# Second attention of a two-block transformer kernel: a tile's normalisation statistics taken one step, their aggregate two steps, behind its residual addition

## The reference: what is computed

```
x = x + jnp.tanh(g_xattn[0]) * _L0_xattn_ref(_layernorm(x, axis=-1), ctx_1024, ...)
x = x + jnp.tanh(g_ffn[0]) * _L0_ffn_ref(_layernorm(x, axis=-1), ...)
x = x + jnp.tanh(g_xattn[1]) * _L1_xattn_ref(_layernorm(x, axis=-1), ctx_1024, mask, ...)
x = x + jnp.tanh(g_ffn[1]) * _L1_ffn_ref(_layernorm(x, axis=-1), ...)

def _layernorm(x, axis=-1, eps=1e-05):
    m = jnp.mean(x, axis=axis, keepdims=True)
    v = jnp.var(x, axis=axis, keepdims=True)
    return (x - m) / jnp.sqrt(v + eps)
```

## Time and profile before

| | before |
|---|---|
| median of 3 runs | 753.41 us (750.35 to 755.98) |
| the profiled execution, its own time | 759.83 us |
| its span | 758.3 us |
| PE busy | 549.0 us (72%) |
| DVE busy | 416.8 us (55%) |
| POOL busy | 330.2 us (44%) |
| ACT busy | 231.6 us (31%) |
| mean granted TensorE clock | 0.832 of full |

### The profile page before, as it was taken

How to read it: one execution, slowest core, us unless ns; L and a number is a source line. 1 busy time by engine, 2 the same in 40 slices (tenths; PEclk the granted TensorE clock), 3 DMA queues, 4 the chain that set the end, 5 groups by cost and what they waited for, 6 DMA issues and landing times.

```text
span 758.3 us, 16967 instructions
## 1 busy us (share of the span) xinstructions
PE 549.0 (72%) x5388; PEld 433.3 (57%) x5389; DVE 416.8 (55%) x1474; ACT 231.6 (31%) x411; POOL 330.2 (44%) x412
## 2 busy tenths in 40 slices
PE   1587957615699999972798887777861388999950
PEld 1356645501289999862354676666650166999950
DVE  4785386997523333314896467878568511222215
ACT  0221001123044444442622454454531021223210
POOL 6212104777535656634500000070747676666650
PEclk9967695865799999996799997786775699999995
DMA  7911000123222222412755164352324113222219
GB/s 199 269 42 32 26 14 30 49 96 99 74 75 82 77 79 74 140 45 68 238 185 175 51 167 109 108 159 51 70 64 129 46 54 103 79 81 77 72 56 311
DMA packets 70254, 74.97 MB, mean 99 GB/s; under 512 B 12216, under 2 KB 58552, under 8 KB 70120
## 3 DMA queue, kind: packets, MB, share of 16 engines
q1 hardware_dynamic: 55240, 49.64, 23.6%
q0 software_dynamic: 9968, 21.88, 9.2%
q10 hardware_dynamic: 4976, 2.53, 1.2%
HBM read 45.62 MB, written 28.29 MB: 97 GB/s over the span
## 4 chain that ended last, share of the span: by engine, by line
PE 51%; DVE 24%; POOL 8%; issue 8%; DMA 6%; ACT 1%; SPq 1%; POOLq 0%; DVEq 0%; ACTq 0%
PE PS L802 47%; POOL xs L543 5%; DVE XN L1406 3%; DVE stats L1385 3%; DMA work<-ys 3%; DVE X L1380 2%; PE PS L983 2%; DVE work L1845 2%; DVE work L1380 1%; POOL work L591 1%; DVE rtmp L1380 1%; DVE mv L1388 1%; DVE nwt L1380 1%; PE PS L1144 1%; POOL work L598 1%
## 5 line engine op out<-in xcount | busy, mean ns | idle before, releaser
L543 POOL DMA_INDIRECT xs<-pack,adr_i x80 | 78.2, 977 | 194.3 <-ACT pack L1219 138.5
L554 POOL DMA_INDIRECT ys<-work x136 | 132.6, 975 | 33.2 <-issue 33.2
L802 PE MATMUL PS<-w,work 128*128 x1088 | 137.4, 281 | 6.5 <-issue 6.4
L802 PEld LDWEIGHTS PS<-w,work 128*128 128x128 f32 x1088 | 129.4, 195 | 11.5 <-issue 10.2
L802 PE MATMUL PS<-work,w1h 128*128 128x256 f16 (+1 forms) x576 | 97.8, 271 | 3.4 <-issue 2.0
L802 PE MATMUL PS<-work 97*64 97x256 f16 (+5 forms) x608 | 75.7, 317 | 13.8 <-DVE work L1512 7.5
L1380 DVE TENSOR_TENSOR work<-PS,work 128x128 f32<-128x128 f32 (+3 forms) x82 | 32.0, 392 | 94.9 <-PE PS L802 50.6
L802 PE MATMUL PS<-work,w1l 128*128 128x256 f16 (+1 forms) x288 | 78.1, 272 | 0.0
L1277 ACT ACTIVATE work<-PS,b 128x256 f32<-128x256 f32 x128 | 50.3, 475 | 77.0 <-PE PS L802 77.0
L802 PEld LDWEIGHTS PS<-work 97*64 97x64 f16 (+2 forms) x608 | 57.7, 165 | 24.7 <-DVE work L1512 10.8
L802 PE MATMUL PS<-ones 128*128 128x512 f16 x195 | 50.7, 418 | 25.7 <-DVE rows_i L1642 12.4
(11 more groups left out here) (288 smaller groups left out, 858.8 us busy)
## 6 DMA issues: line engine op xcount, KB each, us to landing
work<-ys SPq DMA_DIRECT2D x12, 512.0 KB, 6.0
work<-xs SPq DMA_DIRECT2D x32, 130.0 KB
work<-xs SPq DMA_DIRECT2D x60, 65.0 KB
k_parts<-work SPq DMA_DIRECT2D x24, 128.0 KB, 2.1
w<-k_parts SPq DMA_DIRECT2D x8, 384.0 KB
work<-k_parts SPq DMA_DIRECT2D x32, 96.0 KB
work<-q_parts SPq DMA_DIRECT2D x8, 384.0 KB
work<-q_parts SPq DMA_DIRECT2D x32, 96.0 KB
```

The lines of the kernel that those rows point to most:

```text
L543: g.indirect_dma_start(xs[l], bass.IndirectOffsetOnAxis(adr_i[:, k, T:T + 1], 0), pack_of(l, c)[:, s, k, :].bitcast(U32), None)\
L554: g.indirect_dma_start(ys[l], bass.IndirectOffsetOnAxis(xin[:, q, u, :].bitcast(U32)[:, D:D + 1], 0), yrow[:, q, u, :], None).then_inc(ff[ ...
L802: return t.matmul(o, lhsT, rhs, start=start, stop=stop, skip_group_check=True)
```

## The change

`norm_scale` is cut in two: the statistics, and the inverse square root (`norm_root`, unchanged in itself). In the second attention the statistics of a tile are no longer taken by the group. Behind the residual addition of tile `T` VectorE now issues the `bn_aggr` of tile `T-2` and the `bn_stats` of tile `T-1`, each once. When the step of "norm" comes, only what is left of the group is done (`bn_stats` of the last tile, `bn_aggr` of the last two), and then `norm_root`. Two new semaphores, `x3_stats` and `x3_mv`, order them. The other stages call `norm_scale` as before.

```
                 for T in range(t.start, t.stop):
                     ins = v_.bn_aggr(mv[:, T, :], stats[:, T, :])
                 link(ins)
+                norm_root(t)
+
+            def norm_root(t):
+                w = t.stop - t.start
                 x, y, z = nwt[:, 0, 0:w], rstd[:, t], nwt[:, 1, 0:w]
...
+            taken, kept = [0], [0]
+
+            def take_stats(stop):
+                for T in range(taken[0], stop):
+                    dve.wait_ge(x3_done, T + 1)
+                    v_.bn_stats(stats[:, T, :], X[:, T, 0:D]).then_inc(x3_stats, 1)
+                taken[0] = max(taken[0], stop)
+
+            def keep_stats(stop):
+                for T in range(kept[0], stop):
+                    dve.wait_ge(x3_stats, T + 1)
+                    v_.bn_aggr(mv[:, T, :], stats[:, T, :]).then_inc(x3_mv, 1)
+                kept[0] = max(kept[0], stop)
...
                 if 0 <= T < NT:
                     dve.wait_ge(o_ps, T + 1)
                     tt(X[:, T, :], X[:, T, :], PS[:, 6, 0:DE], ALU.add).then_inc(x3_done, 1)
+                    keep_stats(T - 1)
+                    take_stats(T)
...
                 for k in route_at("norm", g):
                     dve.wait_ge(x3_done, group(1, k).stop)
-                    norm_scale(group(1, k))
+                    take_stats(group(1, k).stop)
+                    keep_stats(group(1, k).stop)
+                    dve.wait_ge(x3_mv, group(1, k).stop)
+                    norm_root(group(1, k))
                     route_lg(1, k)
```

More of the change, by code:

```diff
@@ L287, in build @@
         x_plus = sem("x_plus")
+        x3_stats, x3_mv = sem("x3_stats"), sem("x3_mv")
         scat = [[sem(f"scat{l}_{u}") for u in range((4, 2)[l])] for l in range(2)]
```

## The result

The changed kernel takes a median of 749.62 us (743.84 to 757.14, 20 executions); the kernel before, executed again beside it, takes 755.44 us (750.35 to 760.13, 20 executions). The ratio is 0.9939 with a 95% interval of 0.9917 to 0.9960, that is 4.6 us faster, between 3.0 and 6.3; by the two medians it is 5.8. Forecast were 4.07 us, 749.3 us after, and "within 1%" with 0.86. The forecast held. That 749.3 lies so close to 749.62 is partly luck: it was counted from 753.41, the median of three executions, and with twenty the kernel before stands 2 us higher.

What follows compares the result with a forecast made beforehand. GpSimd's 32 scatters were taken to bound the kernel from chunk 4 on, so three groups of five counted: 1.09 + 1.39 + 1.59 = 4.07 us. From 753.4 us that gave 749.3 us, range 747.5 to 751.

Steps and rivals of the forecast that it cites:

- What a group frees: VectorE at each full group's norm: 2.34 us of statistics shrink to 0.485, freeing 1.86 us.
- What a pair costs: One inserted bn_stats and bn_aggr on VectorE: 0.265 us if they overlap as in the burst, 0.425 if not.
- Plain steps cover the pairs: Steps 17 to 20: VectorE waits for TensorE, so pairs are covered, at the tightest all but 0.03 us.
- First group: Norm before step 13: TensorE gains 0.4 us at once, VectorE's maximum 1.55; 1.09 us remain at step 16's heads.
- Second and third group: Second: 1.39 us gained by step 24's heads; third: 1.59 us by the first scatter of chunk 4.
- The waits: TensorE's heads in steps 13, 21 and 29 wait 0.5, 0.9 and 1.6 us; steps 16 and 24 keep some 3.
- GpSimd bounds the end: From chunk 4, 32 back-to-back scatters bound the stage, so nothing is counted for groups 3 and 4.
- Every pair is paid: Rival: no inserted pair is covered or overlaps, costing 8.5 us against 5.6 gained; 2.9 us slower, 756.3 us; chance 0.10.
- the change frees nothing: Rival: TensorE's half-clock stretches lengthen by as much as VectorE gives; 753 to 755 us; chance 0.06.
- Another wait takes the place: Rival: ScalarE's copy limits TensorE after all three norms, each giving 0.43 us; 752.1 us; chance 0.12.
- The clock gives more: Rival: shorter waits keep TensorE at full clock behind norms, 1.5 us more per stretch, 744.7 us with all three; chance 0.20.

Runs made afterwards that it cites:

- three pairs: The changed kernel with every inserted bn_stats and bn_aggr of the plain steps issued three times; 755.66 us, ratio 1.0000 to the kernel before.
- second profile of the change: The changed kernel itself, executed again as the measure for the runs beside it; 751.27 us, ratio 0.9909 to the kernel before.
- groups 3 and 4 alone: The kernel before with only the last two groups (tiles 24 to 31) taking statistics behind the residuals; 756.46 us, ratio 1.0028.
- groups 0 to 2 alone: The changed kernel with only tiles 0 to 23 taking statistics behind the residuals, the last two groups keeping bursts; 750.75 us, 0.9935 of the kernel before.
- the products: TensorE multiplies ones into a free bank during waits: on the changed kernel 747.89 and 747.20 us, on the kernel before 752.80 us.

## Why the prediction was right, point by point

**What a group frees.** Forecast 1.86 us, measured 1.80 in each of three groups. The remaining stretch is 0.54 us and not 0.485: the two aggregates last 0.30 together and start 0.21 behind the statistics, where 0.276 and small gaps had been put. Nothing in it was of another kind.

**What a pair costs.** Forecast 0.265 where it is on the path, measured 0.26 in steps 16 and 24, three times the same with three pairs, and 0.45 for a pair and a lone `bn_stats` together against 0.465. The Trainium skill ("VectorE: DVE Perf Modes", The DRAIN you can't avoid) would have the next operation wait until the pipe of the one before is empty, semaphore or not, but adds that an operation that is not held starts earlier, which the prediction left out. This case's traces show the earlier start, with 0.27 us for two operations of 0.17 and 0.26 us.

**Plain steps cover the pairs.** Mostly right. Step 20, the tight one, took 3.42 us from heads to heads before and 3.43 after, though it has a pair more; with three pairs it took 3.69. With three pairs about 4.6 us went, where the three steps named on the path and the two lone statistics account for about 2.3 (two more of each: 2 x 2 x 0.45 + 2 x 0.26), and the plain steps without cover for the rest, if the middle of the interval is the truth. Which of them pays wasn't taken apart.

**First group.** One step of the prediction was wrong here, the one with ScalarE's copy. The copy that ends at 470.28 was taken for one that the heads of step 13 need, so that TensorE could gain only 0.43 us at once. By the program the heads in step `g` read the copy that ScalarE makes in step `g-1` (`pe.wait_ge(av_sb, T + 1)` with `T` = `g-2`); the later copy is first needed by the transposition behind the heads. A second profile of the change shows it: there the heads of step 13 start before the copy of that step does.

```profile
465.63 1.08 PE L803 MATMUL PS<-ident,work 128*64 128x36 f32 x16
...
465.76 0.38 ACT L1326 ACTIVATE work<-PS 128x256 f32<-128x256 f32 x1 [0.73 <-PE PS L803]
```

What limits TensorE at this place is its own work. In that second profile it ran steps 12 and 13 at half clock (granted 0.50; in the profile before it was 0.54), and the heads of step 13 gained 0.90 us, just the 0.89 that they had waited. In the profile after it ran them at the full clock, and the whole freed time came through (1.82 us). VectorE's part of the chain was forecast rightly: by the heads of step 16 the second profile has gained 1.10 us, where 1.09 was forecast. In the profile after it is 1.99, of which 1.80 - 0.20 - 0.26 = 1.34 us is the change and the rest clock. So the wrong step did not touch the sum, which went on from VectorE's 1.55 and not from TensorE's 0.43: that is luck.

**Second and third group.** Forecast 1.39 and 1.59; with 1.80 for what is freed and the prices of 0.46 and 0.26 it is 1.34 and 1.54. The sum by measured terms is 1.34 + 1.34 + 1.54 = 4.22 us, or 3.98 with the 1.10 of the second profile. The ratio gives 4.6 (3.0 to 6.3), the medians 5.8.

**The waits.** Forecast 0.5, 0.9 and 1.6 us for the heads of steps 13, 21 and 29. The profile has 1.41, 0.84 and none. Only the second is as forecast. In step 13 TensorE, at the full clock, came earlier and waited longer; in step 29, at half clock since step 28 (where, by the place, it had waited 1.97 us for the transfer of the row maxima; the row names no releaser), it came so late that VectorE was done (in the second profile of the change it waited 0.75). A wait is the difference of two arrivals, and the forecast had moved only VectorE's. That steps 16 and 24 keep some 3 us was right: 3.40 and 3.39.

**GpSimd bounds the end.** Right: groups 3 and 4 alone bring nothing, and from the first of the 32 scatters to the last it takes 39.6 to 40.7 us in all 13 profiles.

**The rivals.** "Every pair is paid" and "the change frees nothing" fell. "Another wait takes the place" fell, since the heads don't wait for that copy. "The clock gives more" is half true: the price named, 1.5 us for a stretch, is what the products bring back in steps 21 to 24; but the change by itself doesn't reliably win it. In the profile after, the full clock was won in one stretch and lost in another. From the heads of step 13 to chunk 4 the kernel before and the one with groups 3 and 4 alone took 90.56 and 90.88 us at a granted clock of 0.76 and 0.74; the two profiles of the change and the one with groups 0 to 2 alone took 84.57 to 85.54 at 0.79 to 0.82. That is 5.0 to 6.3 us less, where the measured terms explain 2.4 (3.60 freed, 1.18 for the operations inserted; 3.3 where the heads of step 13 had come late). The rest goes with the clock; that the change brings it is suggested by these five profiles and not shown. The Trainium skill ("TensorE: Matmul & The Clock Gate", HAM clock gate) says that activity releases the clock; the traces agree in the main, with 1.00 granted where six products of 1.47 us together filled part of the wait and 0.55 where nothing did, though 0.60 once stood behind the same six products.

## What to carry to other kernels

A batch of small statistics that stands between two dependent engines is worth taking apart item by item: what it frees is the whole batch less the last item, as far as the engine behind it was really waiting (0.90 of 1.80 us arrived where TensorE itself was late), and what it costs is the price of one item, in the few steps where that item lies ahead of something awaited. Put the item behind the result that others wait for, not ahead of it. And count only the batches ahead of the stage that bounds the end; behind it the same edit is worth nothing.

## What was unexpected of the hardware

Two profiled executions of kernels whose medians differ by 5.8 us can differ by 8.4, since a half-clock stretch (1.5 us each) or the wait of step 12 (none to 2.05 us) falls differently. A stretch between two landmarks tells a quarter of a microsecond where the clock is the same in both profiles: steps 14 to 16, heads to heads, took 10.93 and 10.94 us at the full clock with a pair ahead of the heads, and 10.65 to 10.67 in the four full-clock profiles without one. The median of a dozen executions tells three. Where the clock differs the stretch is no better: steps 21 to 24 took from 16.75 to 18.26 us with the same code.

Thirty-one products whose result nobody reads made the kernel 3.4 us faster with the change and 4.8 without it, in the medians. They stand where TensorE mostly had to wait anyway; what they buy is the clock of the products that follow.
